# A state-space loop on one core: two silus by one ScalarE function each, two additions moved to TensorE, one moved from GpSimd to VectorE

## What is computed

```python
xz = seq @ W_in.T                      # group-normalized x
u, z = split(xz, 2)                    # 128 channels each
u = silu(sum(u_pad[:, k:k+L] * conv_w[:, k] for k in range(4)) + conv_b)
x_dbl = u @ W_x.T                      # dt (4), B (16), C (16)
dt = softplus(x_dbl[..., :4] @ W_dt.T + b_dt)
for t:                                 # 16 states per channel
    h = exp(dt_t * A) * h + (dt_t * u_t) * B_t
    y_t = sum over states of h * C_t
y = (y + u * Dp) * silu(z)
x = x + y @ W_out.T
```

## Time and profile before

| | |
|---|---|
| median of three timed runs | 5961.64 us |
| profiled execution: span from first to last instruction | 5964.8 us (no other time of its own is given) |
| state-space loop in it, first to last product | 77.3 to 3705.1 us |
| busy share of the span, PE / DVE / ACT / POOL | 85% / 82% / 56% / 80% |

### The profile page before, as it was taken

The page is one execution under the profiler, slowest core; times in us unless marked ns, Lnnn a source line. Parts: engine busy times, 40 slices in busy tenths (PEclk is TensorE's granted clock), DMA queues, the critical chain, the costliest instruction groups (busy, mean ns, idle before and its releaser), DMA issues. The chain is left out here.

```text
span 5964.8 us, 72306 instructions
## 1 busy us (share of the span) xinstructions
PE 5055.2 (85%) x22486; PEld 2628.2 (44%) x22486; DVE 4905.1 (82%) x6723; ACT 3368.7 (56%) x4188; POOL 4796.9 (80%) x2195
## 2 busy tenths in 40 slices
PE   6888888888888888888888887884659989899897
PEld 2334333343343333433433333631436656566565
DVE  7999999999999999999999998302876676776665
ACT  4555656656656556555555553100547767677776
POOL 5999999999999999999999998101437767667675
PEclk9999999999999999999999999797789999999999
DMA  5555555555655655555556554195569999999999
GB/s 181 197 206 199 199 201 201 203 201 198 209 199 198 209 196 205 199 198 205 199 198 208 196 203 173 64 402 173 118 131 188 188 168 187 177 177 188 186 187 210
DMA packets 1421378, 1152.35 MB, mean 193 GB/s; under 512 B 1213242, under 2 KB 1223122, under 8 KB 1413204
## 3 DMA queue, kind: packets, MB, share of 16 engines
q1 hardware_dynamic: 1416664, 1148.30, 67.8%
q10 hardware_dynamic: 4478, 1.25, 0.2%
HBM read 814.23 MB, written 21.09 MB: 140 GB/s over the span
## 5 line engine op out<-in xcount | busy, mean ns | idle before, releaser
L871 POOL TENSOR_TENSOR mamba_state<-mamba_state,mamba_c_row 128x1024 f32<-128x1024 f32 x1024 | 2407.5, 2366 | 67.7 <-DVE mamba_state L831 60.4
L705 PE MATMUL mamba_y_ps<-mamba_state,ident 128*128 128x512 f32 x4096 | 1992.5, 612 | 41.1 <-POOL mamba_state L871 40.2
L831 DVE TENSOR_TENSOR_SCAN mamba_state<-mamba_decay,mamba_b_ps 128x1024 f32<-128x1024 f32 x704 | 1608.3, 2285 | 78.9 <-ACT mamba_b_ps L787 1.5
L2009 POOL TENSOR_TENSOR l3s_el<-l3s_s_sb,l3s_eh 128x1024 f16<-128x1024 f32 x512 | 1090.5, 2142 | 507.1 <-ACT l3s_s_sb L1994 499.4
L705 PEld LDWEIGHTS mamba_y_ps<-mamba_state,ident 128*128 128x128 f32 x4096 | 781.3, 195 | 866.2 <-issue 681.1
L2017 DVE TENSOR_SCALAR_CACHE_REDUCE l3s_s_sb<-l3s_s_ps 128x512 f32<-128x512 f32 x1024 | 705.2, 690 | 401.8 <-PE l3s_s_ps L1953 381.2
L787 ACT ACTIVATE mamba_decay<-mamba_dt,mamba_A 128x1016 f32<-128x1016 f32 x704 | 791.5, 1133 | 235.9 <-POOL mamba_dt L852 166.9
L1966 PE MATMUL l3s_o_ps<-l3s_vt,l3s_et 128*128 128x257 f16 x4096 | 810.1, 276 | 91.5 <-DMA l3s_et<-l3s_el 74.1
L817 DVE TENSOR_TENSOR mamba_b_ps<-mamba_dtu,mamba_b_ps 128x1024 f32<-128x1024 f32 x704 | 849.9, 1207 | 30.8 <-PE mamba_b_ps L693 30.6
L1993 ACT ACTIVATE l3s_eh<-l3s_s_sb,l3s_shift 128x1024 f16<-128x1024 f32 x512 | 584.3, 1141 | 411.1 <-DMA l3s_et<-l3s_el 314.2
L693 PE MATMUL mamba_b_ps<-mamba_bc,mamba_pick 128*128 128x512 f32 x1408 | 575.1, 491 | 284.1 <-DVE mamba_state L831 277.4
(11 more groups left out here) (328 smaller groups left out, 5686.9 us busy)
## 6 DMA issues: line engine op xcount, KB each, us to landing
mamba_c_row<-mamba_c_rows SPq DMA_DIRECT2D x1024, 512.0 KB, 3.8
mamba_b_row<-mamba_c_rows SPq DMA_DIRECT2D x320, 512.0 KB, 4.8
l_ring_a<-in_L_conv_W SPq DMA_DIRECT2D x28, 1024.0 KB, 10.9
l2b_ring_b<-in_L_conv_W SPq DMA_DIRECT2D x26, 1024.0 KB, 10.9
mamba_xs<-X SPq DMA_DIRECT2D x64, 256.0 KB, 5.5
l_ring_a<-in_L_conv_W SPq DMA_DIRECT2D x14, 704.0 KB, 12.7
l2b_ring_b<-in_L_conv_W SPq DMA_DIRECT2D x13, 704.0 KB, 12.7
l_ring_a<-in_L_conv_W SPq DMA_DIRECT2D x14, 640.0 KB, 12.1
```

The source lines that it names most:

```text
L705: last = nc.tensor.matmul(y_ps[:, half(h)], C["ident"][:, :], state[:, s % STATES, half(h)], start=False, stop=(s == S - 1))
L831: nc.vector.tensor_tensor_scan(state[:, s % STATES, :], by, add, 0.0, ALU.mult, ALU.add).then_inc(s_scan, 1)
L871: nc.gpsimd.tensor_tensor(state[:, s % STATES, :], state[:, s % STATES, :], c_row[:, s % C_ROWS, :], ALU.mult).then_inc(s_hc, 1)
L2009: nc.gpsimd.tensor_tensor(el[:, part, off:off + EXPW], s_sb[:, par, j * EXPW:(j + 1) * EXPW], eh[:, part, off:off + EXPW], ALU.subtract).t ...
```

## The change

- silu(u) and silu(z) become one ScalarE `Silu` each, written straight to `u` (now double-buffered) and `sz`. Before each the table of functions is loaded, after each that of Exp and Ln is loaded again. Four VectorE and ScalarE passes a silu go.
- The low part of B and C: TensorE adds minus the copy onto the product in PSUM (a matmul with minus the identity, at k=6), and ScalarE copies the result. VectorE's L801 goes.
- X: TensorE turns it from `X` itself (no `xs`, no DMA), adds it in `pe_out` by a matmul with the identity, and ScalarE copies the sum to X in unit 15. VectorE's L840 goes.
- The dt sum goes from GpSimd to VectorE, at k=12, between the drive and the scan of unit 12.

The five GpSimd drives stay. The core of the diff:

```diff
             if k == 0:
-                wait(pe, s_xs, 16 * (n + 1))
...
-                                               xs[:, 2 * j * F:2 * (j + 1) * F], C["ident"][:, :])
+                                               X[:, first + 2 * j * F:first + 2 * (j + 1) * F], C["ident"][:, :])
...
+            if k == 6:
+                wait(pe, s_hi, n + 1)
+                wait(pe, s_cc, n + 1)
+                for h in range(2):
+                    last = nc.tensor.matmul(prep_ps[:, half(h)], C["minus"][:, :], bc[:, par, half(h)], start=False, stop=True,
+                                            skip_group_check=True)
+                last.then_inc(s_rest, 1)
...
+            nc.tensor.matmul(prep_ps[:, 0:COLS], C["ident"][:, :], X[:, columns(c)], start=True, stop=False)
             for n in range(CHUNK_N):
...
-                nc.scalar.activation(gu[:, :], prep_ps[:, :], ACT.Exp, scale=-1.0,
-                                     bias=weights(n)["neg_conv_b"][:, 0:1]).then_inc(s_gu, 1)
-                wait(act, s_gu, 3 * n + 1)
-                nc.scalar.activation(gu[:, :], gu[:, :], ACT.Ln, bias=1.0).then_inc(s_gu, 1)
-            if k == 4:
-                wait(act, s_gu, 3 * n + 2)
-                nc.scalar.activation(gu[:, :], gu[:, :], ACT.Exp, scale=-1.0).then_inc(s_gu, 1)
+                wait(act, s_y, S * (n - 2) + 1)
+                wait(act, s_dtu, n - 1)
+                nc.scalar.activation(u[:, par, :], prep_ps[:, :], ACT.Silu,
+                                     bias=weights(n)["conv_b"][:, 0:1]).then_inc(s_u, 1)
+                act.preload_act_table_set(EXP_LN_TABLES)
...
+            if k == 6:
+                wait(act, s_rest, n + 1)
+                nc.scalar.activation(bc[BLOCK:2 * BLOCK, par, :], prep_ps[BLOCK:2 * BLOCK, :], ACT.Copy).then_inc(s_lo, 1)
...
+        def act_add(act, c):
+            wait(act, s_out, c + 1)
+            nc.scalar.activation(X[:, columns(c)], prep_ps[:, 0:COLS], ACT.Copy).then_inc(s_add, 1)
...
         def dve_prep(dve, n, par, k):
...
+            if k == 12:
+                wait(dve, s_log1p, n + 1)
+                wait(dve, s_pos, n + 1)
+                nc.vector.tensor_tensor(dt[:, par, :], ln_e[:, :], dt[:, par, :], ALU.add).then_inc(s_dt, 1)
...
-            if k == 12:
-                wait(pool, s_log1p, n + 1)
-                wait(pool, s_pos, n + 1)
-                nc.gpsimd.tensor_tensor(dt[:, par, :], ln_e[:, :], dt[:, par, :], ALU.add).then_inc(s_dt, 1)
```

More of the change, by code:

```diff
@@ L454, in _ @@
                 copy_turned(1)
+                nc.vector.tensor_scalar(C["minus"][:, :], C["ident"][:, :], -1.0, None, ALU.mult)
                 dve.wait_ge(s_done, 3)
@@ L670, in pe_prep @@
                 for h in range(2):
-                    last = nc.tensor.matmul(prep_ps[:, half(h)], weights(n)["w_bc"][:, :], u[:, half(h)], start=True, stop=True)
+                    last = nc.tensor.matmul(prep_ps[:, half(h)], weights(n)["w_bc"][:, :], u[:, par, half(h)], start=True, stop=True)
                 last.then_inc(s_pbc, 1)
+            if k == 6:
[5 more added lines that the diff above has]
+                last.then_inc(s_rest, 1)
             if k == 7:
-                wait(pe, s_cc, n + 1)
                 wait(pe, s_lo, n + 1)
                 for h in range(2):
-                    last = nc.tensor.matmul(prep_ps[:, half(h)], weights(n)["w_dt"][:, :], u[:, half(h)], start=True, stop=True)
+                    last = nc.tensor.matmul(prep_ps[:, half(h)], weights(n)["w_dt"][:, :], u[:, par, half(h)], start=True, stop=True)
                 last.then_inc(s_pdt, 1)
             if k == 10:
+                wait(pe, s_ln, n + 1)
                 wait(pe, s_lost, n + 1)
@@ L701, in pe_sum @@
                 for h in range(2):
-                    nc.tensor.matmul(y_ps[:, half(h)], weights(c)["diag_Dp"][:, :], u[:, half(h)], start=True, stop=False)
+                    nc.tensor.matmul(y_ps[:, half(h)], weights(c)["diag_Dp"][:, :], u[:, par, half(h)], start=True, stop=False)
             wait(pe, s_hc, unit + 1)
@@ L725, in act_prep @@
                 wait(act, s_pz, 2 * n)
+                wait(act, s_pu, 2 * n)
                 image = n // PER_IMAGE
@@ L834, in dve_gate @@
             wait(dve, s_y, S * (c + 1))
+            wait(dve, s_sz, c + 1)
             wait(dve, s_out, c)
             nc.vector.tensor_tensor(yz[:, :], sz[:, par, :], y_ps[:, :], ALU.mult).then_inc(s_yz, 1)
-        def dve_add(dve, c):
-            wait(dve, s_out, c + 1)
-            nc.vector.tensor_tensor(X[:, columns(c)], X[:, columns(c)], prep_ps[:, 0:COLS],
-                                    ALU.add).then_inc(s_add, 1)
         def pool_prep(pool, n, par, k):
@@ L910, in sp_unit @@
                 write_c(sp, c + 1, 1 - par)
-            if s == LOAD_AT and prep and c + 2 < TOTAL:
-                load_xs(sp, c + 2)
         def pe_unit(pe, c, par, s, prep):
@@ L930, in act_both @@
                 act_prep(act, c + 1, 1 - par, s)
+            if s == ADD_AT and not is_first(c):
+                act_add(act, c - 1)
         def dve_unit(dve, c, par, s, prep):
@@ L937, in dve_unit @@
                 dve_prep(dve, c + 1, 1 - par, s)
-            if s == ADD_AT and not is_first(c):
-                dve_add(dve, c - 1)
             dve_scan(dve, c, par, s)
@@ L2272, in program @@
         with Memory(nc, "mamba") as m:
+            C["minus"] = m.sb("minus", [P, P], fp32r)
             C["pick"] = m.sb("pick", [P, len(DVE_UNITS) * P], fp32r)
```

58 lines of the change are left out of this document (14 added, 44 removed).

## The result

The changed kernel takes 6115.45 us (median of 4 runs, 6111.42 to 6116.48), the kernel before, timed beside it, 5964.06 us (4 runs, 5961.43 to 5969.36). The ratio is 1.0248, 95% interval 1.0234 to 1.0263: slower by 2.5%, where 6085 us and 2.1% were forecast. The profiled execution has a span of 6114.1 us, 149.3 us more than before's 5964.8.

The account below looks back on a forecast made before the run. GpSimd and VectorE were taken to hand the bound to each other within each chunk. Loop +103, TensorE's slow clock +25 and prologue -5 gave +123 us on 5961.6, so 6085 us (+2.1%), range 6020 to 6170.

Parts of the forecast that it names:

- The sum waits out product 11: Unit 12, VectorE: the dt sum stands until GpSimd's product 11 ends, 2.33 us, then runs 1.02 us.
- The loop through both engines: From log1p to the next log1p through VectorE and GpSimd: 58.43 us a chunk against 56.79, +103 us in 63 chunks.
- TensorE's slow clock: Half speed after TensorE's idle stretch makes unit 15's row spread late: 0.4 us a chunk (bounds 0 and 0.9), +25 us.
- Prologue: Before the loop: silu(u) some 6 us earlier, the longer low part gives 1 back, -5 us.
- Covers: ScalarE's table loads, silus and longer low part cost 0, inside VectorE's slack of 2.9 us a chunk.
- the sum gets in first: Rival, unit 12: VectorE's sum starts before product 11 and takes 1.22 us; loop 56.25 us, 5923 us; chance 0.10.
- they cancel: Rival: the sum starts before product 11, but VectorE waits 0.5 us a chunk for TensorE; 5955 us; chance 0.04.
- GpSimd's relief comes through: Rival: waits on both sides find cover, GpSimd's 23 instructions set 53.6 us a chunk; 5806 us; chance 0.04.
- The stalls add up: Rival: each chunk loses 0.9 us to the slow clock and 0.7 to unit 2's gate; 6161 us or more; chance 0.09.

Follow-up runs that it names:

- one_sbuf: Changed kernel with the dt sum's second input read from PSUM instead of SBUF (z product times 0, relu term left out): 5961.62 us, ratio 0.9991 to the kernel before.
- log_in_psum: Changed kernel reordered: logarithm written to PSUM, VectorE adds relu and logarithm in step 11, GpSimd then subtracts the lost part: 5844.63 us, ratio 0.9793 to the kernel before.
- pool_waits: Changed kernel with one added wait: GpSimd waits for the dt sum before product 11: 5957.28 us, ratio 0.9982 to the kernel before.
- busy_pe: Changed kernel with five more TensorE matmuls a chunk, of a zero matrix, in unit 13: 6066.87 us, ratio 1.0160 to the kernel before.
- sum_back: Changed kernel, but with the dt sum kept on GpSimd at k=12: 5913.38 us, ratio 0.9904 to the kernel before.
- change_late_copy: Changed kernel with ScalarE's copies of B and C moved behind unit 6's decay: 6118.41 us, ratio 1.0251 to the kernel before.
- late_copy_busy: log_in_psum with the copies of B and C behind unit 6's decay and four zero-matrix TensorE matmuls a chunk in unit 11: 5797.99 us, ratio 0.9713 to the kernel before.

## Why the prediction was right

*The sum waits out product 11*: right in size and in place. 3.35 us were forecast (2.33 + 1.02), 3349 ns is the median. That it is the second SBUF input, and who starts first, is shown by one_sbuf (with log_in_psum) and pool_waits, which each change one of the two and bring 1.22 and 1.23 us. This is as the Trainium skill, SBUF — State Buffer, section "Who interferes with whom", has it: a VectorE instruction with at most one SBUF input (outside the modes in which it takes both ports) keeps clear of GpSimd, one with two is held up by a GpSimd instruction that came first and reads SBUF. The traces agree with both halves, 1.22 and 3.35 us.

*The loop through both engines*: 58.43 us forecast, 58.34 measured where TensorE doesn't disturb it (busy_pe). In 63 chunks that is 98 us where the sum had 103.

*TensorE's slow clock*: the term of the sum that was mis-sized. Between bounds of 0 and 0.9 us a chunk I took 0.4, +25 us. It is 0.92, 63 x 0.92 = +58 us. The step that failed is "0.6 us late if the 1.8 us of the earlier trace rows are lost": the slow stretch there held one group of matmuls, so I priced one. In the changed kernel the spread and the matmul for X can be slow too. In the chunk above that is 1.22 for 0.72, 3.62 for 1.88 and 1.75 for 1.02 (the second numbers from busy_pe), 3.0 us in all; the mean over the chunks is 0.47 + 1.44 + 0.28 = 2.2 us, as the stretch is often shorter. With 2.2 in place of 1.8, the same working puts the spread of unit 15 2.2 - 1.2 = 1.0 us late; VectorE waited 53.9 / 63 = 0.86 us a chunk. And "nearer to the lower end since the loss needs the whole slow stretch" was the wrong choice between the ends: the stretch does vary, but the sum was slow in every chunk, and VectorE waited for a row spread in 56 places.

*Prologue*: -5 forecast, -5.15 measured. With 98 and 58 that makes 151 us, against 149.3 in the spans.

*Covers*: the loads of tables, the silus and the longer low part were costed at nothing, under VectorE's slack ahead of log1p. In sum_back hardly anything of them is on the path (its GpSimd waits 24.0 us for scans in the whole loop). In the changed kernel busy_pe leaves no room for them, 58.34 us against a loop of 58.43 without them, and change_late_copy shows that even 1.8 us a chunk ahead of scan 6 cost nothing.

*The rivals*: "the sum gets in first" and "they cancel" describe what pool_waits brings about by its added wait. With 36.5 / 63 = 0.58 us a chunk of waiting for spreads it came to 5957 us, next to the 5955 of the second. "GpSimd's relief comes through" needed 23 instructions a chunk without a late scan; it took another order of the computation and cover for TensorE's idle stretch (late_copy_busy, 5798 us, where 5806 was the rival's time), and doesn't come from the move alone. "The stalls add up" had the slow clock right, at 0.9, but the gate did not add its 0.7 (VectorE's gate waited once in the loop, 4.5 us): the measured time lies between it and the forecast.

## What to carry to other kernels

When an operation is moved off the bounding engine, look first at who it will run beside: an addition of two SBUF tiles on VectorE, started just after a GpSimd instruction that reads SBUF, cost that instruction's rest on top of its own time here, and whoever waited for VectorE paid it. A wait that lets VectorE go first, or a PSUM input, took back 158 and 154 us of the 202 that the moved sum cost. And price a slow clock by all the work that stands behind the idle time, over many chunks, not by the one slow row that a trace happens to show.

## What the hardware showed beyond that

A hand-over by semaphore lost against the next instruction of the engine that handed over, where that was ready: log1p's end released VectorE's sum in 62 of 64 places, and product 11 started before the sum in all 63 chunks of the loop, by 0.08 us in the chunk shown. In 62 of them the sum took over 3.3 us.

TensorE's granted clock stayed up for matmuls with a matrix of zeros: 1.00 in place of 0.76 over 14 us, with five of them a chunk in the idle stretch. Useless work on an engine that idles made two kernels faster, by 49 and by 30 us.

Kernels of equal time can hide very different chains: pool_waits, one_sbuf and the kernel before lie within 9 us of one another, with GpSimd waits for scans of 119, 188 and 60 us (and 85 more for the sum in pool_waits).
